# Mixture of experts: 512-column widening products over four tiles of tokens, with narrowing per pair of tiles

## The chip, the cores and the metric

The kernel runs on one core of a Trainium2 chip. Its metric is the device time of one execution in microseconds (us). Three runs of the kernel before gave 1331.83, 1327.61 and 1333.07 us; the median is 1331.83 us.

## What is computed

The kernel is a two-layer decoder on 32 sequences of 64 tokens with 256 features: 2048 rows, which are 16 tiles of 128 tokens. The change is in the last part, a mixture of 8 experts:

```
h    = layernorm(x)
gate = silu(h @ Wg[e])      # 256 -> 256, for each expert e
mid  = gate * (h @ Wu[e])   # 256 -> 256
x   += zone[:, e] * (mid @ Wd[e])   # 256 -> 256, all experts, weighted by the router
```

Experts 0 and 1 have low-rank terms added to their weights (`Ga @ Gb`, and so on). The router (a sigmoid, a zone test and a fallback on the two largest) gives `zone`.

## The kernel before

The engines run programs of their own and meet at semaphores. PE multiplies, ACT (ScalarE) and DVE (VectorE) work on the results, POOL (GpSimd) prepares rounding remainders, SP issues DMAs. The last part is the function `mixture` (line 2433).

Every product there is made in three passes (`three_passes`, line 1921): both operands are split into a high part, rounded to fp32r, and a low part, the remainder. The passes are high by high, low by high, high by low. Each pass is one weight load and one matmul.

The work goes in 64 steps, `STEPS`: 8 experts by 8 pairs of tiles (a pair has 256 tokens). Step `s` belongs to expert `s // 8` and pair `s % 8`. One step on PE is:

- `widen(s)`, line 2819: for both halves `f` of the 256 middle features, the gate and the up product of the pair's 256 tokens; 2 halves x 2 matrices x 2 chunks of features x 3 passes = 24 matmuls of 256 columns. The moving operand is the transposed input (`xT_high`, `xT_low`), the stationary one the expert's weights. Each half has a PSUM bank of its own (four in a ring): gate in its first 256 columns, up in the last.
- `narrow(s - 2)`, line 2842: the down product of the step before the last (`LAG` is 2): 2 tiles x 2 halves x 3 passes = 12 matmuls of 256 columns.

Between the two stand four elementwise operations for each half `j` (two in each step): ACT takes `silu` of the gate half of the bank (line 2587); DVE multiplies it with the up half into `mid` (line 2721); ACT rounds `mid` to `mid_high` (line 2574); DVE makes the remainder `mid_low` (line 2726). ACT's program issues `silu(j)` and then `middle_high(j - 1)`; DVE's issues `middle(j)` and then `middle_low(j - 1)`. So the last two operations on a half are issued only behind the first two of the next half, and those wait for that next half's products. `narrow(s)` waits for the semaphore `mid_lows`, which counts the `middle_low` operations, to reach `2 (s + 1)`: both halves of its own step. DVE also adds the weighted result of `narrow` to `x` (`add`, line 2735; from expert 1 on), three steps late, ahead of the step's `middle`.

The order is written out by hand: the loop over `s` in each engine's program is the order of its instructions. In the first steps other work stands between: `turn_x` (transposes of the normalised input of a pair), `route_x` (router products), `fold` (low-rank products, two in each of steps 4, 5 and 6). ACT copies each transposed pair (`keep_xT`), DVE rounds it (`x_high`), POOL makes its remainder (`x_low`), and `widen` of the first expert waits for that of its pair.

Of the kernel before, what the change touches and what calls it, by code (L numbers as in the profile page):

```python
# [40 lines left out]
class Core:  # L41
# [10 lines left out]
    def sb(self, name, shape, dtype=F32):  # L52
        return self.ctx.enter_context(self.nc.sbuf_tensor(name, shape, dtype))
# [2379 lines left out]
def mixture(core):  # L2433

    nc, dram, ps, ident = core.nc, core.dram, core.psum, core.ident
    with ExitStack() as scope:  # L2436
# [9 lines left out]
        w_route = sb("w_route", [P, KC, M_EXPERTS])  # L2446
        temperature, first = sb("temperature", [P, 1]), sb("first", [P, M_EXPERTS])
        xn, xT = sb("xn", [P, 4, 2, E]), sb("xT", [P, 4, KC, 2 * P])
        xT_high, xT_low = sb("xT_high", [P, PAIRS, KC, 2 * P], F32R), sb("xT_low", [P, PAIRS, KC, 2 * P], F32R)
        logits, gate, dist, zone, near, rank, hot1, hot2 = (  # L2450
            sb(name, [P, TILES, M_EXPERTS]) for name in ("logits", "gate", "dist", "zone", "near", "rank", "hot1", "hot2"))
        total, nobody, best = (sb(name, [P, TILES]) for name in ("total", "nobody", "best"))
        silu, mid = sb("silu", [P, 4, 2 * P]), sb("mid", [P, 4, 2 * P])
        lora_a, lora_b = (scope.enter_context(nc.sbuf_tensor(f"mo_{name}", [M_RANK, MATRICES, M_LORA, M_FF], F32))
                          for name in ("lora_a", "lora_b"))
        lora = sb("lora", [P, M_LORA, MATRICES, KC, M_FF])
        held = sb("held", [P, PAIRS, 2 * E])
        mid_high, mid_low = sb("mid_high", [P, 4, FT, 2 * P], F32R), sb("mid_low", [P, 4, FT, 2 * P], F32R)
# [16 lines left out]
        def down_bank(s):  # L2475
            return HELD_BANK if s < PAIRS else 4 + s % 4

        def adds_until(s):

            return 2 * (s - PAIRS) + 2  # L2480

        block = scope.enter_context(nc.Block())

# [27 lines left out]
        @block.gpsimd  # L2511
        def _(pool):
            def x_low(p):
                pool.wait_ge(xT_highs, p + 1)
                pool.wait_ge(xT_ready, p + 1)
                nc.gpsimd.tensor_tensor(xT_low[:, p], xT[:, p % 4], xT_high[:, p].bitcast(F32), ALU.subtract).then_inc(xT_lows, 1)  # L2516
# [13 lines left out]

            for p in range(1, PAIRS):
                x_low(p)
            for e in range(1, M_EXPERTS):
                if M_ORDER[e] < M_LORA:
                    add_lora(e)
                weights_low(e)

        @block.scalar
        def _(act):
# [31 lines left out]

            def middle_high(j):
                act.wait_ge(mid_ready, j + 1)
                nc.scalar.copy(mid_high[:, j // FT % 4, j % FT], mid[:, j % 4]).then_inc(mid_highs, 1)

            weight_high(0, GATE)
            keep_xT(0)
# [3 lines left out]
            keep_xT(1)  # L2581
            for s in range(STEPS):
                e, p = s // PAIRS, s % PAIRS
                for f in range(FT):
                    j = FT * s + f
                    act.wait_ge(wide_psum, j + 1)
                    nc.scalar.activation(silu[:, j % 4], ps[:, j % 4, 0:2 * P], ACT.Silu).then_inc(silu_ready, 1)  # L2587
                    if j >= 1:
                        middle_high(j - 1)
                if s < 3:  # L2590
                    keep_xT(2 * s + 2)
                    keep_xT(2 * s + 3)
# [19 lines left out]
            middle_high(FT * STEPS - 1)  # L2612

        @block.vector
        def _(dve):
# [9 lines left out]
            def x_high(p):  # L2625
                dve.wait_ge(xT_psum, p + 1)
                dve.wait_ge(xT_ready, p + 1)  # L2627
                nc.vector.tensor_copy(xT_high[:, p].rearrange("p c t -> p (c t)"), ps[:, TURN_BANK + p % 2, :]).then_inc(xT_highs, 1)  # L2628

            def first_low(k):  # L2630
                dve.wait_ge(w_highs, k + 1)
# [86 lines left out]

            def middle(j):
                dve.wait_ge(silu_ready, j + 1)  # L2720
                nc.vector.tensor_tensor(mid[:, j % 4], silu[:, j % 4], ps[:, j % 4, 2 * P:4 * P], ALU.mult).then_inc(mid_ready, 1)  # L2721

            def middle_low(j):
                place = (slice(None), j // FT % 4, j % FT)
                dve.wait_ge(mid_highs, j + 1)
                nc.vector.tensor_tensor(mid_low[place], mid[:, j % 4], mid_high[place].bitcast(F32), ALU.subtract).then_inc(mid_lows, 1)

            def add_held(p):
                dve.wait_ge(held_ready, p + 1)
# [22 lines left out]
            first_low(GATE)  # L2752
            x_high(0)
            dve.wait_ge(xT_highs, 1)
            nc.vector.tensor_tensor(xT_low[:, 0], xT[:, 0], xT_high[:, 0].bitcast(F32), ALU.subtract).then_inc(first_x_low, 1)  # L2755
            first_low(UP)
            normalise(1)
            first_low(DOWN)
# [1 line left out]
            normalise(3)  # L2760
            x_high(1)
            for s in range(STEPS):
                if s >= PAIRS + LAG + 1:
                    add(s - LAG - 1)
                for f in range(FT):
                    j = FT * s + f
                    middle(j)
                    if j >= 1:
                        middle_low(j - 1)
                if s < 3:  # L2770
                    x_high(2 * s + 2)
# [6 lines left out]
            middle_low(FT * STEPS - 1)  # L2778
            for s in range(STEPS - LAG - 1, STEPS):
                add(s)  # L2780

        @block.tensor
        def _(pe):
# [35 lines left out]
            def widen(s):  # L2819
                e, p = s // PAIRS, s % PAIRS  # L2820
                if e == 0:
                    if p == 0:
                        pe.wait_ge(first_x_low, 1)
                    else:
                        pe.wait_ge(xT_lows, p)
                elif p == 0:
                    pe.wait_ge(w_lows, MATRICES * (e - 1) + UP + 1)
                for f in range(FT):
                    j = FT * s + f
                    if j >= 4:  # L2830
                        pe.wait_ge(mid_ready, j - 3)
                    for k in (GATE, UP):
                        if s == 0 and f == 0:
                            pe.wait_ge(first_lows, k + 1)
                        for c in range(KC):
                            columns = slice(f * P, (f + 1) * P)
                            done = three_passes(nc, ps[:, j % 4, 2 * P * k:2 * P * (k + 1)],
                                                (w_high[:, e % RING, k, c, columns], w_low[:, e % RING, k, c, columns]),
                                                (xT_high[:, p, c], xT_low[:, p, c]), start=(c == 0), stop=(c == KC - 1))
                    done.then_inc(wide_psum, 1)  # L2840

            def narrow(s):
                e, p = s // PAIRS, s % PAIRS
                if p == 0:
                    if e == 0:
                        pe.wait_ge(first_lows, MATRICES)
                    else:
                        pe.wait_ge(w_lows, MATRICES * e)
                pe.wait_ge(mid_lows, FT * (s + 1))
                if 1 <= s <= PAIRS:  # L2850
                    pe.wait_ge(held_ready, s)
                if s == PAIRS + 1:
# [4 lines left out]
                    pe.wait_ge(added, adds_until(s - 4))  # L2857
                for u in range(2):
                    for f in range(FT):
                        tokens = slice(u * P, (u + 1) * P)  # L2860
                        done = three_passes(nc, ps[:, down_bank(s), u * E:(u + 1) * E], (mid_high[:, s % 4, f, tokens], mid_low[:, s % 4, f, tokens]),
                                            (w_high[:, e % RING, DOWN, f], w_low[:, e % RING, DOWN, f]), start=(f == 0), stop=(f == FT - 1))
                done.then_inc(down_psum, 1)

            keep_clock(core, 2, 5)
            turn_x(0)
            keep_clock(core, 2, 4)
            for s in range(STEPS):
                widen(s)
                if s == 0:  # L2870
                    turn_x(1)
                if s == 0:
                    route_x(0)
                    route_x(1)
                if 1 <= s < 4:
                    route_x(2 * s)
                    route_x(2 * s + 1)
                if s < 3:
                    turn_x(2 * s + 2)
                    turn_x(2 * s + 3)  # L2880
                if 4 <= s < 7:
                    fold(2 * (s - 4))
                    fold(2 * (s - 4) + 1)
                if s >= LAG:
                    narrow(s - LAG)
            for s in range(STEPS - LAG, STEPS):
                narrow(s)


# [112 lines left out]
```

## Time and profile before

| | |
|---|---|
| median of 3 runs | 1331.83 us |
| the profiled execution's time | 1335.5 us |
| its span in the trace | 1333.4 us |
| mixture, from its first instruction (1031.9) to the span's end | 301.5 us |
| PE busy in the span | 1217.7 us (91%) |
| PE busy from 1046.4 to 1329.0 | 282.6 of 282.6 us |

How to read it: busy time is the time in which an engine has an instruction under way. Matmuls overlap in the pipeline, so that what a matmul costs in a row of them is the distance between two starts, not its duration. "PEclk" is the granted clock of PE, where 1.00 is 2.4 GHz and 0.50 is 1.2 GHz. A bracket at a row's end tells how long the engine sat idle before that instruction and what it had waited for.

### The profile page before, as it was taken

What the parts mean: (1) busy time and instruction counts of PE and PEld (TensorE: products, weight loads), DVE (VectorE), ACT (ScalarE), POOL (GpSimd) and SP (SyncE); (2) the same over time, 40 slices, a digit from 0 to 9 for tenths busy, and PEclk for the clock granted to TensorE, in tenths of its full rate; (3) what the DMA queues carried; (4) which work ended last, traced back from release to release, by engine and by line L of the source; (5) the groups of instructions that cost most, each with busy time, mean ns of one, the idle gap of its engine ahead of it and who ended that gap; (6) DMA issues with size and microseconds to landing.
All of it is one profiled execution on the core that took longest, in us unless ns stands there. A gap on an engine that the chain in (4) does not pass through costs nothing. (4 is left out here: it accounts for less than half of the span.)

```text
span 1333.4 us, 27527 instructions
## 1 busy us (share of the span) xinstructions
PE 1217.7 (91%) x9976; PEld 967.8 (73%) x9976; DVE 959.4 (72%) x1862; ACT 709.4 (53%) x1475; POOL 454.4 (34%) x537
## 2 busy tenths in 40 slices
PE   5999997989888779798899999999997899999998
PEld 3777764444444557697677878788786899999998
DVE  5889987888887376786567778687775668555555
ACT  2778863878778545000466565656653463333332
POOL 2344642454543124575552423323230201112210
PEclk9999998999999988899999999999999999999999
DMA  5111151133331200001300000000000300000001
GB/s 172 36 36 37 42 149 34 41 81 94 80 92 33 74 41 0 1 0 29 119 9 4 4 8 4 8 4 8 4 1 2 95 25 25 25 25 25 1 1 64
DMA packets 58660, 51.04 MB, mean 38 GB/s; under 512 B 9064, under 2 KB 50888, under 8 KB 58184
## 3 DMA queue, kind: packets, MB, share of 16 engines
q1 hardware_dynamic: 58574, 49.88, 13.3%
q8 instruction: 56, 0.92, 0.3%
q14 instruction: 30, 0.25, 0.1%
HBM read 37.93 MB, written 11.53 MB: 37 GB/s over the span
## 5 line engine op out<-in xcount | busy, mean ns | idle before, releaser
L208 DVE TENSOR_REDUCE stacks_neg_max<-psum 128x2 f32<-128x512 f32 x256 | 163.6, 684 | 39.2 <-PE psum L204 38.6
L952 ACT ACTIVATE fa_probs<-psum 128x1024 f32<-128x1024 f32 x128 | 130.3, 1020 | 46.1 <-PE psum L1069 45.3
L1921 PE MATMUL psum<-mo_xT_high,mo_w_high 128*128 128x256 f32 x512 | 145.2, 284 | 2.8 <-DVE mo_xT_low L2755 2.7
L1921 PE MATMUL psum<-mo_xT_low,mo_w_high 128*128 128x256 f32 x512 | 145.0, 283 | 0.0
L1921 PE MATMUL psum<-mo_xT_high,mo_w_low 128*128 128x256 f32 x512 | 144.2, 282 | 0.0
L2587 ACT ACTIVATE mo_silu<-psum 128x256 f32<-128x256 f32 x128 | 49.0, 384 | 155.0 <-PE psum L1921 155.0
L2721 DVE TENSOR_TENSOR mo_mid<-mo_silu,psum 128x256 f32<-128x256 f32 x128 | 53.6, 419 | 92.9 <-ACT mo_silu L2587 92.8
L204 PE MATMUL psum<-stacks_k_stack,stacks_q_stack 48*128 48x256 bf16 x512 | 89.7, 281 | 16.9 <-DVE stacks_neg_max L208 7.8
L2057 POOL TENSOR_TENSOR ga_probs<-ga_probs,ga_top 128x1024 f32<-128x1024 f32 x16 | 30.5, 1905 | 205.4 <-DVE ga_top L2211 205.4
L1921 PEld LDWEIGHTS psum<-mo_xT_high,mo_w_high 128*128 128x128 f32 x512 | 97.0, 189 | 3.2 <-DVE mo_xT_low L2755 2.8
L1921 PEld LDWEIGHTS psum<-mo_xT_low,mo_w_high 128*128 128x128 f32 x512 | 97.1, 190 | 0.0
L1921 PEld LDWEIGHTS psum<-mo_xT_high,mo_w_low 128*128 128x128 f32 x512 | 97.0, 189 | 0.0
L2528 POOL TENSOR_TENSOR mo_w_low<-mo_raw,mo_w_high 128x512 fp32r<-128x512 f32 x21 | 27.6, 1315 | 188.1 <-ACT mo_w_high L2562 188.1
L1069 PE MATMUL psum<-stacks_q_stack,stacks_k_stack 51*128 51x256 bf16 x512 | 87.5, 280 | 0.2 <-DMA stacks_q_stack<-fa_max_rows 0.2
L2046 POOL TENSOR_TENSOR ga_q_scaled<-ga_q,ga_q_inv 128x1024 f32<-128x1024 f32 x32 | 70.1, 2190 | 38.5 <-ACT ga_q_inv L2088 38.5
L204 PEld LDWEIGHTS psum<-stacks_k_stack,stacks_q_stack 48*128 48x128 bf16 x512 | 32.5, 95 | 69.3 <-DVE stacks_neg_max L208 37.9
L2081 ACT ACTIVATE ga_q_scaled<-ga_q 128x512 f32<-128x512 f32 x64 | 40.3, 632 | 61.8 <-DVE ga_q L2184 61.8
L1081 PE MATMUL psum<-fa_probs,fa_values 128*32 128x256 f32 x1024 | 70.0, 392 | 2.5 <-ACT fa_probs L952 0.4
L1921 PE MATMUL psum<-mo_w_high,mo_mid_high 128*128 128x256 f32 x256 | 72.3, 282 | 0.0
L1921 PE MATMUL psum<-mo_w_low,mo_mid_high 128*128 128x256 f32 x256 | 71.9, 281 | 0.0
L1921 PE MATMUL psum<-mo_w_high,mo_mid_low 128*128 128x256 f32 x256 | 71.7, 280 | 0.0
L2384 PE MATMUL psum<-ga_w_o_high,ga_mixedT_high 128*128 128x256 f32 x256 | 64.7, 293 | 4.9 <-DVE ga_mixedT_low L2203 4.9
(434 smaller groups left out, 3562.3 us busy)
## 6 DMA issues: line engine op xcount, KB each, us to landing
k_parts<-da_k_parts SPq DMA_DIRECT2D x96, 64.0 KB, 2.0
stacks_k_stack<-k_parts SPq DMA_DIRECT2D x32, 192.0 KB
q_parts<-stacks_parts SPq DMA_DIRECT2D x48, 64.0 KB, 2.0
stacks_q_stack<-q_parts SPq DMA_DIRECT2D x32, 96.0 KB
x<-in_x SPq DMA_DIRECT2D x4, 512.0 KB, 7.4
da_context<-in_ctx SPq DMA_DIRECT2D x4, 512.0 KB, 6.9
stacks_q_stack<-q_parts SPq DMA_DIRECT2D x32, 64.0 KB
fa_context<-in_ctx SPq DMA_DIRECT2D x16, 128.0 KB, 2.1
```

Source lines behind the costliest of these rows:

```text
L204: return core.nc.tensor.matmul(core.psum[:, bank, q * E:(q + 1) * E], self.q_stack[lane, slot, b, h // LANES, q * P:(q + 1) * P], self.k_s ...
L208: return core.nc.vector.tensor_reduce(self.neg_max[:, b, :, head_at(h)], core.psum[:, bank, :].rearrange("p (q k) -> p q k", q=2), AX.X, A ...
L952: nc.scalar.activation(probs[:, g].rearrange("p h k q -> p h (k q)"), ps[:, 2 + 2 * (g % 2):4 + 2 * (g % 2), :], ACT.Exp).then_inc(exp_don ...
L1069: return nc.tensor.matmul(ps[:, 2 + h % 4, k * E:(k + 1) * E], k_stack[lane, slot, b, h // LANES, k * P:(k + 1) * P], q_stack[lane, slot, ...
L1081: done = nc.tensor.matmul(ps[32 * c:32 * c + 32, 6, half * E:(half + 1) * E], values[:, slot, k, 8 * b + head_at(h), :], probs[:, h // 2, ...
L1921: done = nc.tensor.matmul(out, lhsT[i], rhs[j], start=start and k == 0, stop=stop and k == 2)
L2046: nc.gpsimd.tensor_tensor(q_scaled[:, columns].rearrange("p (h d) -> p h d", d=G_HD), q[:, columns].rearrange("p (h d) -> p h d", d=G_HD), ...
L2057: nc.gpsimd.tensor_tensor(probs[:], probs[:], top[:, :, None].to_broadcast([P, G_HEADS, SEQ]), ALU.subtract).then_inc(shifted, 1)
L2081: nc.scalar.activation(q_scaled[:, g * G_CHUNK:(g + 1) * G_CHUNK], q[:, g * G_CHUNK:(g + 1) * G_CHUNK], ACT.Square).then_inc(squares_ready, 1)
L2384: nc.tensor.matmul(ps[:, 6, 0:E], mixedT_high[:, h], weight[:, h], start=(h == 0 and weight is w_o_high), stop=False)
L2587: nc.scalar.activation(silu[:, j % 4], ps[:, j % 4, 0:2 * P], ACT.Silu).then_inc(silu_ready, 1)
L2721: nc.vector.tensor_tensor(mid[:, j % 4], silu[:, j % 4], ps[:, j % 4, 2 * P:4 * P], ALU.mult).then_inc(mid_ready, 1)
```

## The change

A step is now one half of the middle features for four tiles (512 tokens) instead of both halves for two tiles. There are still 64 steps, and `narrow(s)` still makes the down product of one pair.

```diff
-        xT_high, xT_low = sb("xT_high", [P, PAIRS, KC, 2 * P], F32R), ...
+        xT_high, xT_low = sb("xT_high", [P, PAIRS // 2, KC, 4 * P], F32R), ...
-        silu, mid = sb("silu", [P, 4, 2 * P]), sb("mid", [P, 4, 2 * P])
+        silu, mid = sb("silu", [P, 2, 4 * P]), sb("mid", [P, 4, 4 * P])
-        mid_high, mid_low = sb("mid_high", [P, 4, FT, 2 * P], F32R), ...
+        mid_high, mid_low = sb("mid_high", [P, 2, FT, 4 * P], F32R), ...
...
@@ scalar
-                for f in range(FT):
-                    j = FT * s + f
-                    act.wait_ge(wide_psum, j + 1)
-                    nc.scalar.activation(silu[:, j % 4], ps[:, j % 4, 0:2 * P], ACT.Silu).then_inc(silu_ready, 1)
-                    if j >= 1:
-                        middle_high(j - 1)
+                act.wait_ge(wide_psum, s + 1)
+                nc.scalar.activation(silu[:, s % 2], ps[:, s % 2 * 2 + GATE, :], ACT.Silu).then_inc(silu_ready, 1)
+                if s >= 1:
+                    middle_high(s - 1)
...
@@ vector
-                if s >= PAIRS + LAG + 1:
+                if PAIRS + LAG + 1 <= s < STEPS - 1:
                     add(s - LAG - 1)
-                for f in range(FT):
-                    j = FT * s + f
-                    middle(j)
-                    if j >= 1:
-                        middle_low(j - 1)
+                middle(s)
+                if s >= 1:
+                    middle_low(s - 1)
...
@@ tensor
+            def widen(s, tokens=slice(0, 4 * P)):
+                e, q, f = s // PAIRS, s % PAIRS // 2, s % 2
+                for k in (GATE, UP):
...
+                    for c in range(KC):
+                        columns = slice(f * P, (f + 1) * P)
+                        done = three_passes(nc, ps[:, s % 2 * 2 + k, tokens], ...
+                if tokens.stop == 4 * P:
+                    done.then_inc(wide_psum, 1)
+
+            def whole(s):
                 e, p = s // PAIRS, s % PAIRS
                 if e == 0:
-                    if p == 0:
-                        pe.wait_ge(first_x_low, 1)
-                    else:
-                        pe.wait_ge(xT_lows, p)
+                    pe.wait_ge(xT_lows, p // 2 * 2 + 1)
                 elif p == 0:
                     pe.wait_ge(w_lows, MATRICES * (e - 1) + UP + 1)
...
+                pe.wait_ge(mid_ready, s - 1)
+                widen(s)

             def narrow(s):
...
-                pe.wait_ge(mid_lows, FT * (s + 1))
+                pe.wait_ge(mid_lows, s // 2 * 2 + 2)
...
             for s in range(STEPS):
-                widen(s)
                 if s == 0:
+                    pe.wait_ge(first_x_low, 1)
+                    widen(0, pairs[0])
                     turn_x(1)
-                if s == 0:
+                    widen(1, pairs[0])
                     route_x(0)
+                    pe.wait_ge(xT_lows, 1)
+                    widen(0, pairs[1])
                     route_x(1)
+                elif s == 1:
+                    widen(1, pairs[1])
+                else:
+                    whole(s)
...
-                if s >= LAG:
+                if LAG <= s < STEPS - 2:
                     narrow(s - LAG)
-            for s in range(STEPS - LAG, STEPS):
+            for s in range(STEPS - LAG - 2, STEPS):
                 narrow(s)
```

How the instructions stand. PE in the middle of the stage, where a wide step ends and a `narrow` begins. A name in brackets is the semaphore waited for, under the name that its number had first: `da_top_raw0` is `mid_lows`, `da_shifted0` is `added`. The kernel before:

```order
L1921 MATMUL psum<-mo_xT_high,mo_w_low 128x256
L1921 MATMUL psum<-mo_xT_low,mo_w_high 128x256
L1921 MATMUL psum<-mo_w_high,mo_mid_high 128x256 [waits da_shifted0,da_top_raw0]
L1921 MATMUL psum<-mo_w_high,mo_mid_low 128x256
L1921 MATMUL psum<-mo_w_low,mo_mid_high 128x256
```

and the changed kernel at the same place:

```order
L1921 MATMUL psum<-mo_xT_high,mo_w_low 128x512
L1921 MATMUL psum<-mo_xT_low,mo_w_high 128x512
L1921 MATMUL psum<-mo_w_high,mo_mid_high 128x256 [waits da_shifted0,da_top_raw0]
L1921 MATMUL psum<-mo_w_high,mo_mid_low 128x256
L1921 MATMUL psum<-mo_w_low,mo_mid_high 128x256
```

The position of `narrow` behind a wide step is the same; ahead of it stand 12 matmuls of 512 columns instead of 24 of 256.

DVE in the same stage: `da_keys_ready` is `silu_ready`, `da_scored1` is `mid_highs`. One step of the kernel before:

```order
L2746 SCALAR_TENSOR_TENSOR x<-psum,mo_zone,x 128x256 [waits da_shifted0,da_top_raw1]
L2746 SCALAR_TENSOR_TENSOR x<-psum,mo_zone,x 128x256 [waits da_shifted0]
L2721 TENSOR_TENSOR mo_mid<-mo_silu,psum 128x256 [waits da_keys_ready]
L2726 TENSOR_TENSOR mo_mid_low<-mo_mid,mo_mid_high 128x256 [waits da_scored1]
L2721 TENSOR_TENSOR mo_mid<-mo_silu,psum 128x256 [waits da_keys_ready]
L2726 TENSOR_TENSOR mo_mid_low<-mo_mid,mo_mid_high 128x256 [waits da_scored1]
```

and one step of the changed kernel:

```order
L2751 SCALAR_TENSOR_TENSOR x<-psum,mo_zone,x 128x256 [waits da_shifted0,da_top_raw1]
L2751 SCALAR_TENSOR_TENSOR x<-psum,mo_zone,x 128x256 [waits da_shifted0]
L2727 TENSOR_TENSOR mo_mid<-mo_silu,psum 128x512 [waits da_keys_ready]
L2731 TENSOR_TENSOR mo_mid_low<-mo_mid,mo_mid_high 128x512 [waits da_scored1]
```

A step has one `mid` and one `mid_low` of 512 columns in place of two of each of 256, and the `mid_low` that stands in step `s` is that of step `s - 1`.

## Rows read from the trace of the kernel before

**Rows 1.** Windows: us, busy us per engine, PEclk, DMA share, GB/s
```profile
1200.00:1300.00 100.00, 100.00 (x849) 100.00 (x848) 56.15 (x141) 36.97 (x105) 19.90 (x15) 1.00 0.03 9
```
**Rows 2.** Waits from 930 on: us in total, times, longest
```profile
ACT mo_silu L2587 <- PE psum L1921: 155.0, 121, 2.2
```
**Rows 3.** Timeline, one step on PE: start, us, engine, line, operation
```profile
1088.09 0.28 PE L1921 MATMUL psum<-mo_xT_high,mo_w_high 128*128 128x256 f32 x1
...
1090.93 0.28 PE L1921 MATMUL psum<-mo_w_high,mo_mid_high 128*128 128x256 f32 x1
...
1092.34 0.28 PE L1921 MATMUL psum<-mo_xT_high,mo_w_high 128*128 128x256 f32 x1
```
**Rows 4.** Timeline, 512-column passes of the stage before: first and last of eleven
```profile
889.22 0.39 PE L1921 MATMUL psum<-w_q_high,ga_xT_low 128*128 128x512 f32 x1
...
891.54 0.40 PE L1921 MATMUL psum<-w_q_low,ga_xT_high 128*128 128x512 f32 x1
```
**Rows 5.** Timeline, end of a half's products and the work on it
```profile
1323.32 0.28 PE L1921 MATMUL psum<-mo_xT_low,mo_w_high 128*128 128x256 f32 x1
...
1323.64 0.38 ACT L2587 ACTIVATE mo_silu<-psum 128x256 f32<-128x256 f32 x1 [2.15 <-PE psum L1921]
...
1323.92 0.40 ACT L2574 CAST mo_mid_high<-mo_mid 128x256 fp32r<-128x256 f32 x1
...
1324.05 0.42 DVE L2721 TENSOR_TENSOR mo_mid<-mo_silu,psum 128x256 f32<-128x256 f32 x1 [0.96 <-ACT mo_silu L2587]
...
1324.39 0.42 DVE L2726 TENSOR_TENSOR mo_mid_low<-mo_mid,mo_mid_high 128x256 fp32r<-128x256 f32 x1
```
**Rows 6.** Groups by line and form, ACT: busy us, mean ns, idle before
```profile
L952 ACT ACTIVATE fa_probs<-psum 128x1024 f32<-128x1024 f32 x128 | 130.3, 1020 | 46.1 <-PE psum L1069 45.3
L2574 ACT CAST mo_mid_high<-mo_mid 128x256 fp32r<-128x256 f32 x128 | 51.0, 398 | 5.1 <-DVE mo_mid L2721 5.1
L2587 ACT ACTIVATE mo_silu<-psum 128x256 f32<-128x256 f32 x128 | 49.0, 384 | 155.0 <-PE psum L1921 155.0
L2562 ACT CAST mo_w_high<-mo_raw 128x512 fp32r<-128x512 f32 x24 | 14.8, 621 | 2.3 <-DMA mo_raw<-in_mo_w_gate 2.3
```
**Rows 7.** Groups by line and form, DVE, from 1030 on
```profile
L2721 DVE TENSOR_TENSOR mo_mid<-mo_silu,psum 128x256 f32<-128x256 f32 x128 | 53.6, 419 | 92.9 <-ACT mo_silu L2587 92.8
...
L2628 DVE CAST mo_xT_high<-psum 128x512 fp32r<-128x512 f32 x8 | 5.2, 683 | 3.1 <-ACT mo_xT L2550 3.1
...
L2755 DVE TENSOR_TENSOR mo_xT_low<-mo_xT,mo_xT_high 128x512 fp32r<-128x512 f32 x1 | 0.7, 693 | 0.0
```
**Rows 8.** Timeline, a DVE remainder and the PE products that waited for it
```profile
1037.71 0.69 DVE L2755 TENSOR_TENSOR mo_xT_low<-mo_xT,mo_xT_high 128x512 fp32r<-128x512 f32 x1
...
1038.46 0.39 PE L1921 MATMUL psum<-mo_xT_high,mo_w_high 128*128 128x256 f32 x1 [2.65 <-DVE mo_xT_low L2755]
1038.68 0.28 PE L1921 MATMUL psum<-mo_xT_high,mo_w_low 128*128 128x256 f32 x1
1038.81 0.28 PE L1921 MATMUL psum<-mo_xT_low,mo_w_high 128*128 128x256 f32 x1
```
**Rows 9.** Timeline, PE in step 4: last wide product, folds, narrowing
```profile
1067.52 0.28 PE L1921 MATMUL psum<-mo_xT_low,mo_w_high 128*128 128x256 f32 x1
1067.72 1.99 PE L2815 MATMUL psum<-mo_lora_b,mo_lora_a 64*128 64x256 f32 x8
1069.65 0.39 PE L1921 MATMUL psum<-mo_w_high,mo_mid_high 128*128 128x256 f32 x1
```
**Rows 10.** Timeline, two other PE waits
```profile
1008.95 0.58 PE L2384 MATMUL psum<-ga_w_o_high,ga_mixedT_high 128*128 128x256 f32 x1 [2.53 <-DVE ga_mixedT_low L2203]
...
1023.71 0.39 PE L2384 MATMUL psum<-ga_w_o_high,ga_mixedT_high 128*128 128x256 f32 x1 [2.37 <-DVE ga_mixedT_low L2203]
```
**Rows 11.** Windows behind the three waits; the last but two is PEclk
```profile
1008.90:1012.20 3.30, 3.25 (x15) 3.25 (x16) 3.29 (x6) 1.06 (x1) 0.41 (x1) 0.50 0.02 5
1023.70:1027.10 3.40, 3.39 (x28) 3.39 (x29) 1.52 (x4) 0.00 (x0) 0.00 (x0) 1.00 0.00 0
1039.50:1042.90 3.40, 3.40 (x18) 3.40 (x17) 2.05 (x6) 0.00 (x0) 0.00 (x0) 0.50 1.04 250
```

More of the change, by code:

```diff
@@ L2448, in mixture @@
         xn, xT = sb("xn", [P, 4, 2, E]), sb("xT", [P, 4, KC, 2 * P])
-        xT_high, xT_low = sb("xT_high", [P, PAIRS, KC, 2 * P], F32R), sb("xT_low", [P, PAIRS, KC, 2 * P], F32R)
+        xT_high, xT_low = sb("xT_high", [P, PAIRS // 2, KC, 4 * P], F32R), sb("xT_low", [P, PAIRS // 2, KC, 4 * P], F32R)
         logits, gate, dist, zone, near, rank, hot1, hot2 = (
@@ L2457, in mixture @@
         held = sb("held", [P, PAIRS, 2 * E])
-        mid_high, mid_low = sb("mid_high", [P, 4, FT, 2 * P], F32R), sb("mid_low", [P, 4, FT, 2 * P], F32R)
+        mid_high, mid_low = sb("mid_high", [P, 2, FT, 4 * P], F32R), sb("mid_low", [P, 2, FT, 4 * P], F32R)
         loaded, lora_loaded, xn_ready, xT_psum, xT_ready, xT_highs, xT_lows, routed, logits_ready, route_step, inverted = (
@@ L2480, in adds_until, with of_pair, of_middle @@
             return 2 * (s - PAIRS) + 2
+        def of_pair(half, p):
+            return half[:, p // 2, :, p % 2 * 2 * P:(p % 2 + 1) * 2 * P]
+        def of_middle(half, j):
+            return half[:, j // FT % 2, j % FT]
         block = scope.enter_context(nc.Block())
@@ L2515, in x_low @@
                 pool.wait_ge(xT_ready, p + 1)
-                nc.gpsimd.tensor_tensor(xT_low[:, p], xT[:, p % 4], xT_high[:, p].bitcast(F32), ALU.subtract).then_inc(xT_lows, 1)
+                nc.gpsimd.tensor_tensor(of_pair(xT_low, p), xT[:, p % 4], of_pair(xT_high, p).bitcast(F32), ALU.subtract).then_inc(xT_lows, 1)
             def add_lora(e):
@@ L2573, in middle_high @@
                 act.wait_ge(mid_ready, j + 1)
-                nc.scalar.copy(mid_high[:, j // FT % 4, j % FT], mid[:, j % 4]).then_inc(mid_highs, 1)
+                nc.scalar.copy(of_middle(mid_high, j), mid[:, j % 4]).then_inc(mid_highs, 1)
             weight_high(0, GATE)
@@ L2611, in _ @@
                     weight_high(e + 1, p - 3)
-            middle_high(FT * STEPS - 1)
+            middle_high(STEPS - 1)
         @block.vector
@@ L2627, in x_high @@
                 dve.wait_ge(xT_ready, p + 1)
-                nc.vector.tensor_copy(xT_high[:, p].rearrange("p c t -> p (c t)"), ps[:, TURN_BANK + p % 2, :]).then_inc(xT_highs, 1)
+                nc.vector.tensor_copy(of_pair(xT_high, p), ps[:, TURN_BANK + p % 2, :].rearrange("p (c t) -> p c t", c=KC)).then_inc(xT_highs, 1)
             def first_low(k):
@@ L2720, in middle @@
                 dve.wait_ge(silu_ready, j + 1)
-                nc.vector.tensor_tensor(mid[:, j % 4], silu[:, j % 4], ps[:, j % 4, 2 * P:4 * P], ALU.mult).then_inc(mid_ready, 1)
+                nc.vector.tensor_tensor(mid[:, j % 4], silu[:, j % 2], ps[:, j % 2 * 2 + UP, :], ALU.mult).then_inc(mid_ready, 1)
             def middle_low(j):
-                place = (slice(None), j // FT % 4, j % FT)
                 dve.wait_ge(mid_highs, j + 1)
-                nc.vector.tensor_tensor(mid_low[place], mid[:, j % 4], mid_high[place].bitcast(F32), ALU.subtract).then_inc(mid_lows, 1)
+                nc.vector.tensor_tensor(of_middle(mid_low, j), mid[:, j % 4], of_middle(mid_high, j).bitcast(F32), ALU.subtract).then_inc(mid_lows, 1)
             def add_held(p):
@@ L2754, in _ @@
             dve.wait_ge(xT_highs, 1)
-            nc.vector.tensor_tensor(xT_low[:, 0], xT[:, 0], xT_high[:, 0].bitcast(F32), ALU.subtract).then_inc(first_x_low, 1)
+            nc.vector.tensor_tensor(of_pair(xT_low, 0), xT[:, 0], of_pair(xT_high, 0).bitcast(F32), ALU.subtract).then_inc(first_x_low, 1)
             first_low(UP)
@@ L2777, in _ @@
                     route(s - 4)
-            middle_low(FT * STEPS - 1)
-            for s in range(STEPS - LAG - 1, STEPS):
+            middle_low(STEPS - 1)
+            for s in range(STEPS - LAG - 2, STEPS):
                 add(s)
@@ L2817, in fold @@
                 done.then_inc(folded_psum, 1)
-            def widen(s):
+            def widen(s, tokens=slice(0, 4 * P)):
+                e, q, f = s // PAIRS, s % PAIRS // 2, s % 2
+                for k in (GATE, UP):
+                    if s == 0 and tokens.start == 0:
+                        pe.wait_ge(first_lows, k + 1)
+                    for c in range(KC):
+                        columns = slice(f * P, (f + 1) * P)
+                        done = three_passes(nc, ps[:, s % 2 * 2 + k, tokens],
+                                            (w_high[:, e % RING, k, c, columns], w_low[:, e % RING, k, c, columns]),
+                                            (xT_high[:, q, c, tokens], xT_low[:, q, c, tokens]), start=(c == 0), stop=(c == KC - 1))
+                if tokens.stop == 4 * P:
+                    done.then_inc(wide_psum, 1)
+            def whole(s):
                 e, p = s // PAIRS, s % PAIRS
                 if e == 0:
-                    if p == 0:
-                        pe.wait_ge(first_x_low, 1)
-                    else:
-                        pe.wait_ge(xT_lows, p)
+                    pe.wait_ge(xT_lows, p // 2 * 2 + 1)
                 elif p == 0:
                     pe.wait_ge(w_lows, MATRICES * (e - 1) + UP + 1)
[L2828 to L2840, printed above, removed]
+                pe.wait_ge(mid_ready, s - 1)
+                widen(s)
             def narrow(s):
@@ L2859, in narrow @@
                     for f in range(FT):
-                        tokens = slice(u * P, (u + 1) * P)
-                        done = three_passes(nc, ps[:, down_bank(s), u * E:(u + 1) * E], (mid_high[:, s % 4, f, tokens], mid_low[:, s % 4, f, tokens]),
+                        tokens = slice((s % 2 * 2 + u) * P, (s % 2 * 2 + u + 1) * P)
+                        done = three_passes(nc, ps[:, down_bank(s), u * E:(u + 1) * E],
+                                            (mid_high[:, s // 2 % 2, f, tokens], mid_low[:, s // 2 % 2, f, tokens]),
                                             (w_high[:, e % RING, DOWN, f], w_low[:, e % RING, DOWN, f]), start=(f == 0), stop=(f == FT - 1))
@@ L2867, in _ @@
             keep_clock(core, 2, 4)
+            pairs = slice(0, 2 * P), slice(2 * P, 4 * P)
             for s in range(STEPS):
-                widen(s)
                 if s == 0:
+                    pe.wait_ge(first_x_low, 1)
+                    widen(0, pairs[0])
                     turn_x(1)
-                if s == 0:
+                    widen(1, pairs[0])
                     route_x(0)
+                    pe.wait_ge(xT_lows, 1)
+                    widen(0, pairs[1])
                     route_x(1)
+                elif s == 1:
+                    widen(1, pairs[1])
+                else:
+                    whole(s)
                 if 1 <= s < 4:
@@ L2883, in _ @@
                     fold(2 * (s - 4) + 1)
-                if s >= LAG:
+                if LAG <= s < STEPS - 2:
                     narrow(s - LAG)
-            for s in range(STEPS - LAG, STEPS):
+            for s in range(STEPS - LAG - 2, STEPS):
                 narrow(s)
```

## The prediction

> **What bounds the kernel now.** I read the table of windows first. In the mixture's steady part PE is busy all the time, at the full granted clock (PEclk 1.00 of 2.4 GHz), while DVE is busy half of it and ACT a third [rows 1]. The list of waits confirms it from the other side: ACT waited 155.0 us for PE's products, and nobody waits long for anything else [rows 2]. So the stage's time is PE's issue time, and two questions remain: what do the new products cost, and does PE still find its operands ready.
>
> The timeline of one step gives the issue time [rows 3]: 24 wide matmuls take 1090.93 - 1088.09 = 2.84 us (118.3 ns each), 12 narrow ones 1092.34 - 1090.93 = 1.41 us (117.5 ns). A step is 4.25 us.
>
> **Part 1: 512 columns instead of 256.** The stage before has the same kind of pass with 512 columns: ten distances in 891.54 - 889.22 = 2.32 us, 232 ns each [rows 4]. Two passes of 256 cost 236.6 ns. A wide step becomes 12 x 0.232 = 2.784 us, a gain of 0.056 us; over 62 steps that are wholly wide, **-3.5 us**. Half the weight loads and half the instructions are gone, and yet the gain is small, because the time goes by columns. Bounds: at 228 ns it is -6.5 us, at 236 ns nothing (the rows show single distances of 0.22 to 0.24 us).
>
> **Part 2: what PE now waits for.** This decides. `narrow(t)` waits until `mid_lows` is `t // 2 * 2 + 2`. For odd `t` that is `t + 1`, its own step's remainder, long made. For even `t` it is `t + 2`: the pair's second half of features is made by step `t + 1`. PE issues `narrow(t)` right behind `whole(t + 2)`. So at every even step `s` PE needs `mid_low(s - 1)` as soon as `whole(s)` is issued. But DVE issues `middle_low(s - 1)` behind `middle(s)`, that waits for `silu(s)`, and that for the last product of `whole(s)` itself. Before, the same pattern was harmless: `narrow(s - 2)` needed the remainder of half `2s - 3`, issued in step `s - 1`, a whole step earlier. Now PE must stand through three elementwise operations in a row.
>
> I price the wait from the last product's start, T:
> - T to the start of `silu`: the chain at 256 columns shows 1323.64 - 1323.32 = 0.32 us with a product of 0.28 us, so 0.04 us behind its end [rows 5]. A 512-column product lasts 0.39 us [rows 4]: T + 0.43.
> - `silu` of 512: between 384 ns at 256 and 1020 ns at 1024 columns for an activation from PSUM [rows 6], 0.60 us. `mid` starts 0.41 us after a `silu` of 0.38 us starts [rows 5], so 0.03 us behind its end: T + 1.06.
> - `mid` of 512: 0.42 us at 256 [rows 7]; a 512-column pass of DVE out of PSUM takes 0.683 us [rows 7]. The following instruction starts 0.08 us before its end (1324.39 - 1324.05 against 0.42) [rows 5]: `mid_low` starts at T + 1.66. `mid_high(s - 1)` is ready by then: ACT starts it 0.28 us after `silu` at 256, 0.1 us before its end [rows 5], here T + 0.93, and it takes 0.62 us like the 512-column cast [rows 6].
> - `mid_low` of 512: 0.693 us, the same operation on `xT` [rows 7]: T + 2.36. PE starts 0.06 us behind such a remainder (1038.46 against 1037.71 + 0.69) [rows 8]: T + 2.42.
>
> Without the wait the next product would start at T + 0.23, so **2.19 us** are lost. To this comes the restart: the first distance behind a wait is 0.22 us instead of 0.12 [rows 8], 0.10 us. Together **2.29 us**.
>
> How many: even steps 2 to 60 (from step 62 on, no `narrow` stands in the loop). At step 2, transposes and router products stand between and cover it. At steps 4 and 6 the two folds cover most: narrowing starts 2.13 us after the last wide product there [rows 9], some 2.24 us with 512 columns, against 2.42; 0.2 us each remain. Steps 8 to 60 are 27 full waits: 27 x 2.29 = 61.8, with the folds **+62.2 us**. Behind the waiting instruction stands all PE work, and no other engine gives the time back, since all wait for PE. Lower bound for one wait 2.0 us, were `mid` and `mid_low` to take 0.6 each (27 x 2.0 = 54); upper 2.6, were each twice its 256-column time of 0.42, with the restart (70).
>
> **Part 3: the clock.** PE stood idle 2.53, 2.37 and 2.65 us at three places [rows 8, 10]. Around the first and the third the granted clock went to 0.50 (1.2 GHz) for about 3.4 us, at the second it stayed at 1.00 [rows 11]. Busy at half speed for 3.4 us costs 1.7 us. The new waits are 2.2 us, a little shorter than all three. The bounds are none of 27 (0) and all of them (46 us). I take a quarter, 7 x 1.7 = **+12 us**: a wait like the one that kept its clock is the nearest, but by 0.2 us only.
>
> **Part 4: the ends.** At the start the products and transposes are the same in number; two more changes between plain fp32 and fp32r work cost 0.1 us each (0.20 against 0.12 at such a change [rows 9]), and DVE's 512-column `mid(0)` stands ahead of the rounding of pairs 2 and 3, so that the next pairs' normalisation, and with it the fourth and fifth transposes, come some 0.4 us later: +0.6, between -0.5 and +2. At the end `narrow(60)` and `narrow(61)` (2.82 us) cover the chain of step 63, which is longer by one operation, 3.2 us against 3.05: +0.1. POOL and SP keep their orders, and their work stays beside PE's.
>
> **Sum.** -3.5 + 62.2 + 12 + 0.7 = +71 us on the profiled execution: 1335.5 to 1407. That execution was 3.7 us above the median of the runs; on 1331.8 the sum is **1403 us**.
>
> **Rivals.**
> - The waits are there but the clock never falls: 1331.8 + 59.4 = 1391 us. For it: the wait of 2.37 us kept the clock [rows 10, 11]. Against: two of three did not.
> - The clock falls at nearly every wait: 1331.8 + 59.4 + 46 = 1437 us. For it: the waits are all alike and come every 10.6 us (2 x 4.2 + 2.2); against, as above, they are shorter than any that lost it.
> - The wide products start much faster than 232 ns, since half of the weight loads are gone, and pay for the waits: not slower than before. The point from which it decides is where 62 steps give back 59.4 + 3.5 = 63 us, 1.02 us a step: 2.84 - 1.02 = 1.82 us for 12, 152 ns each. At 131 ns it would be 62 x (2.784 - 1.57) = 75 us less than in my sum without the clock: 1316 us. Every row of 512 columns speaks against it (eleven starts at 232 ns, with weight loads between) [rows 4]. The Trainium skill, "TensorE: Matmul & The Clock Gate", section "Back-to-back issue gap", gives for a stream of weight loads and matmuls 131 ns a matmul at 512 columns, which is where the 131 comes from. The trace disagrees: 232 ns; the measurement decides.
> - The change does not wait, because something else lets `middle_low(s - 1)` go early. Then parts 1 and 4 alone remain: 1329 us. The order of DVE's instructions leaves no room for that.
>
> **Chances and range.** Waits with some falls of the clock 0.57 (1393 to 1420), waits with none 0.22, waits with nearly all 0.14, a much cheaper wait than priced (1345 to 1380) 0.04, cheap products 0.02, no wait 0.01. The range from 1383 to 1432 leaves out most of the third, the fourth and the last two. A measurement of this kernel can tell about 0.5% from no change, 6.7 us: faster 0.02, same 0.01, slower 0.97.
>
> **What would show it.** In the list of PE's waits a new row, products waiting for `mo_mid_low`, some 60 us in 27 to 30 times, none longer than 2.5 us, at even steps only; a period of two steps of about 10.7 us; 512-column passes 232 ns apart; PE no longer busy all the time, but about 80%; stretches of PEclk below 1.00 in the stage, where there are none after 1043 now. I am wrong on the main step if that row is missing or below 40 us, on the products if their distance is below 225 or above 238 ns, and on the clock if it never falls or falls behind most waits.

## The result and the profile after

The changed kernel takes 1400.08 us, the median of 4 runs (1397.89 to 1405.15), against 1331.91 us before, measured beside it: a ratio of 1.0523, 95% interval 1.0495 to 1.0551. It is 5.2% slower; the forecast was 1403 us.

The stages ahead of the mixture differ from run to run by some us (in the traces the first wide product starts between 1032.2 and 1038.5 us), so below I also compare the **mixture's length**, from its first wide product to its last matmul. Both ends are starts of matmuls. It was 290.5 us before (1038.46 to 1328.98) and is 362.4 us now (1036.29 to 1398.70): +71.9 us. The whole span grew by 69.7 us in the two traces (1333.4 to 1403.1), since the stages ahead took 2.2 us less the second time.

The list of PE's waits in the mixture (engine, tile and line waited for: us in total, times, longest). The first two rows are new; the other two belong to the start and had their counterparts before (2.7 us for `mo_xT_low`, 1.0 us for `mo_xn`):

```profile
PE psum L1921 <- DVE mo_mid_low L2731: 40.5, 20, 2.3
PE psum L1921 <- issue: 14.5, 7, 2.1
PE psum L1921 <- DVE mo_xT_low L2760: 3.1, 1, 3.1
PE psum L2794 <- DVE mo_xn L119: 1.7, 2, 1.0
```

The first two rows belong together: 27 times, 55.0 us in all. For seven of them the profile did not find the releaser, but they stand at the same place in the program, ahead of `narrow` at an even step, and have nearly the same length. The number is the one forecast, 27. The row counts idle time only, 2.04 us each, which begins when the last wide product has ended; by the distance between starts a wait is 2.40 us.

One wait, in the timeline of step 16, to hold against [rows 5]:

```profile
1137.19 0.39 PE L1921 MATMUL psum<-mo_xT_low,mo_w_high 128*128 128x512 f32 x1
1137.61 0.60 ACT L2593 ACTIVATE mo_silu<-psum 128x512 f32<-128x512 f32 x1 [3.08 <-PE psum L1921]
1138.11 0.61 ACT L2582 CAST mo_mid_high<-mo_mid 128x512 fp32r<-128x512 f32 x1
1138.24 0.69 DVE L2727 TENSOR_TENSOR mo_mid<-mo_silu,psum 128x512 f32<-128x512 f32 x1 [1.32 <-ACT mo_silu L2593]
1138.85 0.68 DVE L2731 TENSOR_TENSOR mo_mid_low<-mo_mid,mo_mid_high 128x512 fp32r<-128x512 f32 x1
...
1139.59 0.39 PE L1921 MATMUL psum<-mo_w_high,mo_mid_high 128*128 128x256 f32 x1 [2.01 <-DVE mo_mid_low L2731]
1139.81 0.28 PE L1921 MATMUL psum<-mo_w_high,mo_mid_low 128*128 128x256 f32 x1
```

From the last wide product's start: `silu` at +0.42 (forecast 0.43), `mid` at +1.05 (1.06), `mid_low` at +1.66 (1.66), PE again at +2.40 (2.42), and then 0.22 us to its next product (0.22). The reader should see that `silu`, `mid` and `mid_low` start within 0.1 us of the end of the one before (`mid_high`, on ACT, runs beside `mid` and ends 0.13 us ahead of the start of `mid_low`), and that PE has nothing in between.

The windows, to hold against [rows 1] and [rows 11]: a steady stretch, a stretch behind the wait that ended at 1127.4, one behind the wait that ended at 1139.6, and one in the start. Behind the length of the window stand the busy times of PE, of its weight loads, of DVE, ACT and POOL; the last but two is PEclk.

```profile
1200.00:1300.00 100.00, 81.81 (x439) 68.57 (x438) 39.20 (x75) 24.58 (x46) 15.55 (x12) 0.97 0.05 16
1128.60:1132.00 3.40, 3.40 (x11) 2.82 (x11) 0.88 (x2) 0.00 (x0) 0.00 (x0) 0.50 0.02 5
1139.60:1143.00 3.40, 3.40 (x21) 3.05 (x22) 1.60 (x4) 0.00 (x0) 0.00 (x0) 1.00 0.00 0
1050.10:1053.50 3.40, 3.40 (x13) 3.01 (x14) 3.23 (x7) 1.18 (x2) 0.93 (x1) 0.50 0.02 5
```

PE is busy 82% of the steady stretch instead of all of it. The granted clock fell behind 7 of the 27 waits, each time 0.6 to 1.5 us after the wait had ended (from 1094.5, 1128.6, 1173.0, 1227.6, 1272.0, 1326.6 and 1370.9 on). In the start it is at half twice, from 1036.4 and from 1050.1 on; before it was once, from 1039.5 on [rows 11].

The elementwise operations in groups (mean ns behind the busy time), to hold against [rows 6, 7]:

```profile
L2727 DVE TENSOR_TENSOR mo_mid<-mo_silu,psum 128x512 f32<-128x512 f32 x64 | 44.0, 687 | 149.0 <-ACT mo_silu L2593 149.0
L2731 DVE TENSOR_TENSOR mo_mid_low<-mo_mid,mo_mid_high 128x512 fp32r<-128x512 f32 x64 | 43.9, 686 | 0.1
L2582 ACT CAST mo_mid_high<-mo_mid 128x512 fp32r<-128x512 f32 x64 | 39.1, 611 | 0.2 <-DVE mo_mid L2727 0.2
L2593 ACT ACTIVATE mo_silu<-psum 128x512 f32<-128x512 f32 x64 | 38.3, 598 | 241.2 <-PE psum L1921 241.2
```

All four are within 2% of their estimates (0.683, 0.693, 0.62, 0.60).

### The profile page after: what moved, and what is told of

The parts are those of the page before. It is cut to its first block and busy times, and to the rows that moved or that the text cites. A ratio compares the mean times of both kernels' runs of the same rounds, so it can differ in the third digit from the quotient of the medians.

```text
span 1403.1 us, 25783 instructions
## 1 busy us (share of the span) xinstructions
PE 1230.5 (88%) x9232; PEld 937.6 (67%) x9232; DVE 943.2 (67%) x1734; ACT 693.8 (49%) x1347; POOL 456.2 (33%) x537
## 5 line engine op out<-in xcount | busy, mean ns | idle before, releaser
L2593 ACT ACTIVATE mo_silu<-psum 128x512 f32<-128x512 f32 x64 | 38.3, 598 | 241.2 <-PE psum L1921 241.2
L2727 DVE TENSOR_TENSOR mo_mid<-mo_silu,psum 128x512 f32<-128x512 f32 x64 | 44.0, 687 | 149.0 <-ACT mo_silu L2593 149.0
L1921 PE MATMUL psum<-mo_w_high,mo_mid_high 128*128 128x256 f32 x256 | 75.4, 295 | 55.2 <-DVE mo_mid_low L2731 40.5
L1921 PE MATMUL psum<-mo_xT_high,mo_w_high 128*128 128x512 f32 (+1 forms) x264 | 108.0, 409 | 3.7 <-DVE mo_xT_low L2760 3.1
L1921 PE MATMUL psum<-mo_xT_high,mo_w_low 128*128 128x512 f32 (+1 forms) x264 | 106.4, 403 | 0.0
L1921 PE MATMUL psum<-mo_xT_low,mo_w_high 128*128 128x512 f32 (+1 forms) x264 | 106.0, 402 | 0.0
L1921 PEld LDWEIGHTS psum<-mo_w_high,mo_mid_high 128*128 128x128 f32 x256 | 48.5, 189 | 69.1 <-DVE mo_mid_low L2731 50.3
L2751 DVE SCALAR_TENSOR_TENSOR x<-psum,mo_zone,x 128x256 f32<-128x256 f32 x112 | 48.8, 478 | 43.6 <-PE psum L1921 43.6
L2384 PE MATMUL psum<-ga_w_o_low,ga_mixedT_high 128*128 128x256 f32 x256 | 64.0, 289 | 0.0
```

Of the source, the lines that this page charges most:

```text
L1921: done = nc.tensor.matmul(out, lhsT[i], rhs[j], start=start and k == 0, stop=stop and k == 2)
L2384: nc.tensor.matmul(ps[:, 6, 0:E], mixedT_high[:, h], weight[:, h], start=(h == 0 and weight is w_o_high), stop=False)
L2593: nc.scalar.activation(silu[:, s % 2], ps[:, s % 2 * 2 + GATE, :], ACT.Silu).then_inc(silu_ready, 1)
L2727: nc.vector.tensor_tensor(mid[:, j % 4], silu[:, j % 2], ps[:, j % 2 * 2 + UP, :], ALU.mult).then_inc(mid_ready, 1)
L2751: nc.vector.scalar_tensor_tensor(core.x[:, t, :], ps[:, down_bank(s), u * E:(u + 1) * E], zone[:, t, x:x + 1], core.x[:, t, :], ALU.mult, ...
```

## The experiments

Each was run beside the kernel before.

**One step more between widening and narrowing.**

```diff
-        RAW, RING, LAG, MATRICES = 2, 2, 2, 3
+        RAW, RING, LAG, MATRICES = 2, 2, 3, 3
...
-                if LAG <= s < STEPS - 2:
+                if LAG <= s < STEPS - 1:
                     narrow(s - LAG)
-            for s in range(STEPS - LAG - 2, STEPS):
+            for s in range(STEPS - LAG - 1, STEPS):
                 narrow(s)
```

> The changed kernel with LAG 3 instead of 2: every narrow stands one wide step later, so that PE issues narrow(2k) behind whole(2k + 3), one step after DVE issued the remainder it needs; at the end one narrow moves into the loop. Theory (the wait is for mid_low, by the order of issue, 2.40 us at 27 even steps, and the clock falls are its consequence): the waits vanish, PEclk stays 1.00 behind the start, and the time falls by 27 x 2.29 + 7 x 1.7 = 74 us from 1400, to 1326, or 1324 to 1331. Rival one (the first matmul of narrow really waits for the other semaphore in its list, added, or for down_psum's consumers): the waits stay, 1400. Rival two (the wait only moves to the odd steps or to another operand): 1370 to 1400, with a new row in the list of waits.

Measured: 1327.76 us, ratio 0.9986 (0.9972 to 1.0001). The row of waits for `mo_mid_low` is gone, and PE is busy all the time again:

```profile
1200.00:1300.00 100.00, 100.00 (x575) 87.67 (x574) 49.47 (x96) 31.22 (x57) 20.87 (x15) 1.00 0.03 9
```

The mixture's length is 289.1 us, 73.3 less than in the changed kernel. So the whole loss hangs on where `narrow` stands, and both rivals (the semaphore `added`, a wait that moves to the odd steps) fall. `added` falls because `LAG` shifts DVE's `add` as well: in both kernels the add that `narrow(t)` needs is issued three steps ahead of it, and yet the wait is gone. The clock fell nowhere behind 1052.9 until the work's end.

**The order of issue on ACT and DVE, with the distance left at two steps.**

```diff
@@ scalar
+                if s >= 1:
+                    middle_high(s - 1)
                 act.wait_ge(wide_psum, s + 1)
                 nc.scalar.activation(silu[:, s % 2], ...
-                if s >= 1:
-                    middle_high(s - 1)
@@ vector
-                middle(s)
                 if s >= 1:
                     middle_low(s - 1)
+                middle(s)
```

> The changed kernel with LAG 2 as it is, but ACT issues middle_high(s - 1) ahead of silu(s), and DVE issues middle_low(s - 1) ahead of middle(s). Theory (not the distance of two steps is too short but the order of issue makes mid_low(s - 1) wait for the products of step s): mid_low(s - 1) is ready some 2.5 us behind the end of whole(s - 1), narrow(s - 2) comes 4.2 us behind it, no wait is left: 1324 to 1331, as with LAG 3. Rival (two steps are too short in any order): waits remain at even steps, 1340 to 1400.

Measured: 1332.23 us, ratio 1.0019 (1.0003 to 1.0036); the mixture's length is 292.8 us. 24 of the 27 waits are gone, and three remain:

```profile
PE psum L1921 <- DVE mo_mid_low L2731: 2.6, 3, 1.7
```

The longest is at step 8, where DVE's program has the router's chain of small operations (`route`, until 1088.9) ahead of `mid_low`:

```profile
1088.58 0.29 DVE L2692 TENSOR_TENSOR mo_hot<-mo_rank,mo_best 128x128 f32<-128x128 f32 x1
1088.79 0.68 DVE L2731 TENSOR_TENSOR mo_mid_low<-mo_mid,mo_mid_high 128x512 fp32r<-128x512 f32 x1
...
1089.53 0.39 PE L1921 MATMUL psum<-mo_w_high,mo_mid_high 128*128 128x256 f32 x1 [1.71 <-DVE mo_mid_low L2731]
```

The order of issue is the cause in the steady part, as the theory has it. The expectation of "no wait at all" was too strong, and the time lies just above its 1324 to 1331 us: two steps suffice only where DVE has little else in its program. The other two waits (0.45 and 0.44 us idle, at steps 12 and 14) show it too: there DVE works on `x` for the first expert and the second (1.92 and 0.87 us) ahead of `mid_low`, which starts at 1106.40 and 1115.48, when PE has nearly issued its wide products.

**256 columns against 512, with the waits out of the way.** This run has LAG 3 and:

```diff
                 pe.wait_ge(mid_ready, s - 1)
-                widen(s)
+                widen(s, slice(0, 2 * P))
+                widen(s, slice(2 * P, 4 * P))
```

> The run with LAG 3, but each wide step's products as 24 matmuls of 256 columns (first two tiles, then the other two) instead of 12 of 512; elementwise operations stay at 512 columns. It prices the 512 columns alone. Theory (time goes by columns, 232 against 2 x 118.3 ns): 62 x 0.056 = 3.5 us slower than the run with LAG 3, 2 to 5. Rival (the weight loads matter, by the Trainium skill's rate for streams of weight loads and matmuls): 30 us slower or more. Rival (no difference at all): within 1 us.

Measured: 1333.31 us, ratio 1.0016 (1.0004 to 1.0028), 5.5 us above the run with 512 columns (3.4 above its repeat further down); mixture 293.4 us, 4.3 longer. In the timeline of this run a wide step takes 1099.42 - 1096.57 = 2.85 us:

```profile
1096.57 0.28 PE L1921 MATMUL psum<-mo_xT_high,mo_w_high 128*128 128x256 f32 x1
...
1099.42 0.28 PE L1921 MATMUL psum<-mo_w_high,mo_mid_high 128*128 128x256 f32 x1
```

and in the run with LAG 3 and 512 columns 1097.68 - 1094.90 = 2.78 us:

```profile
1094.90 0.39 PE L1921 MATMUL psum<-mo_xT_high,mo_w_high 128*128 128x512 f32 x1
...
1097.68 0.28 PE L1921 MATMUL psum<-mo_w_high,mo_mid_high 128*128 128x256 f32 x1
```

Products of 512 columns are worth 4 us here, as the distances of [rows 3, 4] said, and nowhere near the 30 of the rival.

**Fillers in the wait.** Plain products of the identity, behind the wait for `added` and ahead of that for `mid_low`:

```diff
-                pe.wait_ge(mid_lows, s // 2 * 2 + 2)
...
+                if s % 2 == 0 and PAIRS - 2 <= s < STEPS - 4:
+                    keep_clock(core, down_bank(s), 12)
+                pe.wait_ge(mid_lows, s // 2 * 2 + 2)
```

> The changed kernel with 12 plain 128 x 128 products of the identity put into the wait at each even step from 8 to 60: they write the PSUM bank that narrow overwrites next, and stand behind the wait for added and ahead of that for mid_low. They take about 12 x 0.11 = 1.3 us of the 2.2 us that PE stands idle. Theory (the clock falls come from the idle time, each costs 1.7 us, and the wait itself is ACT's and DVE's chain and does not shorten): the distance over the wait stays 2.4 us, PEclk stays 1.00 from 1055 on, the time falls by 7 x 1.7 = 12 us, to 1388 (1385 to 1391). Rival (the falls cost nothing, since a slow PE only shortens its wait): 1400. Rival (the fillers delay narrow): 1400 to 1410.

Measured: 1406.31 us, ratio 1.0553 (1.0528 to 1.0578). The size was wrong: each plain fp32 product stands in the trace as two matmuls, so that 12 of them are 24 records and took 2.60 us instead of 1.3:

```profile
1148.69 2.84 PE L77 MATMUL psum<-ident 128*128 128x128 f32 x24
1151.29 0.36 PE L1921 MATMUL psum<-mo_w_high,mo_mid_high 128*128 128x256 f32 x1
```

They delayed `narrow` by 0.43 us (2.83 from the last wide product at 1148.46, against 2.40), 27 times, 11.6 us, and the clock fell behind none of the waits. The two cancel: the mixture's length is 362.9 us. By itself the run is inconclusive on the price of a fall, so I repeated it with 5 products.

> As the run with 12 fillers in the wait, but with 5. Those 12 turned out to be 24 passes and took 2.60 us, 0.4 us longer than the idle time, at every even step. 5 are 10 passes, some 1.1 us, and end before the remainder does. Theory (each fall of the clock costs 1.7 us and comes from the idle time; the wait itself is the chain): distance over the wait 2.40 us as in the changed kernel, no fall of the clock in the steady part, 1400 - 12 = 1388 (1385 to 1392). Rival (the falls cost nothing): 1400. Rival (1.1 us of work are not enough to hold the clock): 7 falls as before, 1400.

Measured: 1391.12 us, ratio 1.0461 (1.0438 to 1.0484); mixture 351.1 us.

```profile
1141.69 0.40 PE L1921 MATMUL psum<-mo_xT_low,mo_w_high 128*128 128x512 f32 x1
1141.92 1.28 PE L77 MATMUL psum<-ident 128*128 128x128 f32 x10
1144.10 0.38 PE L1921 MATMUL psum<-mo_w_high,mo_mid_high 128*128 128x256 f32 x1 [0.90 <-DVE mo_mid_low L2731]
```

The distance over the wait is 2.41 us as in the changed kernel. The fillers stand behind the wait for `added` and start 0.23 us after the last wide product, as any next product does, so that `added` holds nothing up. PEclk stays at 1.00 behind the start:

```profile
1200.00:1300.00 100.00, 91.93 (x549) 80.32 (x548) 40.26 (x76) 24.63 (x45) 17.93 (x13) 1.00 0.05 17
```

So the mixture lost 362.4 - 351.1 = 11.4 us to seven falls, 1.6 us each. The changed kernel's own trace agrees: from one wait's end to the next it takes 12.2 us with a fall (1127.40 to 1139.59) and 10.6 without (1116.78 to 1127.40). Work in a wait that shortens nothing still made the kernel faster by keeping the clock; the intervals of the two ratios (up to 1.0484 with the fillers, from 1.0495 without) don't overlap.

**The order on DVE alone.** The second hunk of the order experiment without the first.

> The changed kernel, LAG 2, with only DVE's order changed: middle_low(s - 1) ahead of middle(s); ACT still issues middle_high(s - 1) behind silu(s). Theory (the wait is the chain of elementwise operations behind the last wide product): the chain is now silu, mid_high, mid_low, with mid out of it: 0.43 + 0.50 + 0.61 + 0.04 + 0.69 + 0.06 = 2.33 us from the last product's start instead of 2.40, so waits of the same size at the same 27 even steps, 27 x 0.07 = 2 us less in all: 1395 to 1402. Rival (the order on DVE alone makes the wait): 1324 to 1335.

Measured: 1397.93 us, ratio 1.0504 (1.0479 to 1.0528). The waits stay:

```profile
1120.41 0.39 PE L1921 MATMUL psum<-mo_xT_low,mo_w_high 128*128 128x512 f32 x1
...
1120.84 0.60 ACT L2593 ACTIVATE mo_silu<-psum 128x512 f32<-128x512 f32 x1 [2.56 <-PE psum L1921]
1121.33 0.61 ACT L2582 CAST mo_mid_high<-mo_mid 128x512 fp32r<-128x512 f32 x1
1121.97 0.69 DVE L2731 TENSOR_TENSOR mo_mid_low<-mo_mid,mo_mid_high 128x512 fp32r<-128x512 f32 x1 [0.86 <-ACT mo_mid_high L2582]
...
1122.72 0.39 PE L1921 MATMUL psum<-mo_w_high,mo_mid_high 128*128 128x256 f32 x1 [1.92 <-DVE mo_mid_low L2731]
```

2.31 us instead of 2.40, by the chain that was put down (2.33). Taking `mid` out of the chain gains next to nothing, since `mid_high` takes its place. What counts is that one member of the chain stands behind `silu(s)`. The clock fell behind five of these 27 waits, not seven; the mixture's length is 357.1 us, 5.3 less than in the changed kernel, most of it by two falls fewer (some 3.2 us) and by the shorter waits.

**A shorter start.** In the start of the changed kernel PE waits twice, 0.60 us for the second pair's remainder and 0.68 us for normalised rows, while DVE stands idle. This run has LAG 3 and:

```diff
@@ vector
+                if s < 2:
+                    normalise(2 * s + 4)
+                    normalise(2 * s + 5)
                 middle(s)
...
-                if s < 2:
-                    normalise(2 * s + 4)
-                    normalise(2 * s + 5)
@@ tensor
                     route_x(0)
+                    route_x(1)
                     pe.wait_ge(xT_lows, 1)
                     widen(0, pairs[1])
-                    route_x(1)
```

> The run with LAG 3 and two moves in the first two steps: DVE normalises pairs 4 and 5 (6 and 7) ahead of middle(s) instead of behind the rounding of the pairs before, in a stretch in which it stood idle 3.76 us; PE makes route_x(1) ahead of the wait for the second pair's remainder instead of behind the products. Theory (the start is longer than before by two waits of PE, 0.83 and 0.95 us between starts, that neither work nor buffers ask for): from the first wide product to the end 1.5 us less than with LAG 3, up to 3 if the clock keeps its level behind 1049: 1324 to 1327. Rival (the operations moved early only shift the wait to the transposes' copies): as with LAG 3, within 0.5 us.

Measured: **1326.07 us, ratio 0.9972 (0.9956 to 0.9988)**, 0.3% faster than the kernel before, and far faster than the changed one. From the first wide product to step 2 it takes 13.0 us instead of 15.2, both waits are gone, the second fall of the clock in the start (from 1049.5 on with LAG 3) does not come, and the mixture's length is 286.2 us, 2.8 less than with LAG 3. The run makes both moves at once and does not tell what each is worth. The run with LAG 3 beside it in the same comparison:

> The run with LAG 3 once more, beside the one with the moved start: 1328, and the same length of the mixture in the trace (289.1 us from the first wide product to the last matmul) within 0.5 us.

Measured: 1329.96 us, ratio 0.9996 (0.9983 to 1.0008), mixture 289.3 us. Its median is 2.2 us above that of its first run; the mixture's length, which leaves out the stages ahead, repeats within 0.3 us.

## Why the prediction was right, step by step

| term | forecast | measured | by |
|---|---|---|---|
| 27 waits with the restart | +61.8 | 27 x (2.42 - 0.23 + 0.10) = +62 | the distances over the waits, mean 2.42 us |
| falls of the clock behind the waits | +12 (7 of 27) | +11.4 (7 of 27) | 5 fillers against the changed kernel |
| 512 columns | -3.5 | -4.3 | LAG 3 with 512 and with 256 columns |
| start | +0.6 (-0.5 to 2) | about +2.8 | timeline, below |
| sum, without folds and end | +71 | +72 | mixture's length: +71.9 |

The run with LAG 3 splits the sum in two, and both halves close: against the changed kernel its mixture is 73.3 us shorter (waits and falls: 62 + 11.4), against the kernel before 1.4 us shorter (columns and start: -4.3 + 2.8).

- **The place and cause of the wait** held: it was read from the order of issue (`middle_low(s - 1)` stands behind `middle(s)`, which waits for the very products that PE has just issued), and moving either end of it, the place of `narrow` or the places of `middle_high` and `middle_low` on both engines, removed it (in the second case all but three of the 27). Moving only `middle_low` did not. At steps 4 and 6, where the folds cover most of the wait, `narrow` came 0.16 us late, forecast 0.2.
- **Its price** held within 0.02 us, since each member was taken from a row with the same or a like operation at 512 columns (for `mid` a cast out of PSUM, 0.683 us against the 0.687 measured), or from two sizes around it, and the joints from rows of the same chain.
- **The clock** came out as taken, but the count by luck. I took a quarter of 27 because one of three waits of nearly this length had kept its clock; waits that look all alike (2.40 to 2.45 us but for the first two) were followed by a fall seven times and by none twenty times, and with DVE's order alone changed 27 waits of 2.31 to 2.36 us (again but for the first two) by five falls. What tells them apart was not tested. The price of a fall, 1.7 us in the forecast, is 1.6.
- **The 512-column products** were right in sign and size.
- **What bounds the kernel** was right, but one reading for it was not: that nobody else waits long. DVE waited 92.9 us for `silu` in the same trace [rows 7], and POOL 188.1 us for `mo_w_high`. PE, which was busy all the time, waited for neither.
- **The start** was mis-sized. Part 4 gave +0.6 us with an upper bound of 2. From the first wide product to step 2 the changed kernel takes 15.3 us (1036.29 to 1051.58), before it took 13.4 (1038.46 to 1051.85): +1.9. And step 2's wide products took 3.74 us, because the clock had fallen at 1050.1; at the full clock, in the run with the shorter start, they take 2.88. So the start cost 1.9 + 0.9 = 2.8 us more than before:

```profile
1042.79 0.39 PE L1921 MATMUL psum<-mo_xT_high,mo_w_high 128*128 128x256 f32 x1 [0.60 <-POOL mo_xT_low L2524]
...
1050.00 1.92 PE L2794 MATMUL psum<-ident,mo_xn 128*128 128x128 f32 x8 [0.68 <-DVE mo_xn L119]
...
1051.58 0.77 PE L1921 MATMUL psum<-mo_xT_high,mo_w_high 128*128 128x512 f32 x1
...
1055.32 0.51 PE L2805 MATMUL psum<-mo_w_route,mo_xT 128*128 128x8 f32 x4
```

  The term that was off is the one that put the delay of the fourth and fifth transposes at 0.4 us. It left out that PE, which now has 36 matmuls in the trace instead of 52 ahead of the second pair's products, reaches the wait for that pair's remainder too early, and it had no fall of the clock in the start: by the transposes at 1050.00 (1.58 us to the next product, 0.82 before) and the wide products behind them that fall alone is 1.6 of the 2.8 us. It is 2 us of 72 here, but it is half of what 512 columns give: with LAG 3 alone the kernel is not measurably faster, with the start mended it is.
- Of the rivals, "no fall of the clock" (1391) is what the run with 5 fillers shows (1391.12), "falls at nearly every wait" did not come, and cheap 512-column products are refuted by 232 ns in the trace of the run with LAG 3 (2.78 us for 12).

## What to carry to other kernels

When work is regrouped, follow each consumer's wait to the place in the producer's program where that operation is issued, and see what stands ahead of it: here a remainder that belonged to step s - 1 was issued behind an operation that waits for step s, and a distance of two steps became none. Larger instructions brought little on PE, whose time here goes by columns (2.78 us for 12 of 512, 2.85 for 24 of 256), while each elementwise operation in the chain behind them became 0.2 to 0.3 us longer. One more step of distance cost no time and gave back all 73 us.

## What the runs showed of the hardware

- The first distance between matmuls behind a wait is about 0.22 us instead of 0.12: 0.19 to 0.23 us behind all 27 waits of the changed kernel, with the same kind of product on both sides of them.
- Waits of 2.0 us idle time can be followed by 3.4 us at half the granted clock: 7 of 27 in the changed kernel, and 5 of 27 of 1.9 us with DVE's order alone changed. Five plain products inside each wait (10 records, 1.28 us, with 0.9 to 1.2 us idle left behind them) kept the clock in all 27. A fall cost 1.6 us.
- Plain fp32 products of 128 x 128 are recorded as two matmuls of 0.108 us each (24 in 2.60 us), so 0.217 us a product, while an fp32r pass of 256 columns takes 0.118.
